# Layer 1's x for three of five groups as wide rows read from DRAM, spreads on TensorE for the other two

## The chip, the cores and the metric

The kernel runs on one core of one Trainium2 chip. The metric is the device time of one execution in microseconds (us). Engines are named as in the profile: PE is TensorE, PEld its weight loads, DVE VectorE, ACT ScalarE, POOL GpSimd, SP SyncE; SPq is the queue of DMAs that SP issues.

## What is computed

A recommendation tower with two layers of feature interaction for a batch of 512, 39 features of 16 numbers each:

```python
e = stack([tbl_f[ids[:, f]] for f in range(39)], axis=1)            # 512 x 39 x 16
z0 = einsum('bid,bjd->bdij', e, e).reshape(B, D, 39 * 39)
cur0 = relu(einsum('bdk,kl->bld', z0, W0))                          # L = 128
next_h, direct0 = split(cur0, 2, axis=1)                            # 64 and 64
z1 = einsum('bid,bjd->bdij', e, next_h).reshape(B, D, 39 * 64)
cur1 = relu(einsum('bdk,kl->bld', z1, W1))
z = sum(concatenate([direct0, cur1], axis=1), axis=-1)              # 512 x 192
h = concatenate([z, dense_ctx], axis=1)
y = relu(relu(h @ W_top1 + b_top1) @ W_top2 + b_top2) @ W_top3
```

The change concerns the products of x with h of layer 1 (`z1`).

## The kernel before

The batch is cut into 16 chunks of 32 rows, so a chunk has N = 32 x 16 = 512 columns. For each chunk POOL issues 11 indirect gathers (L233) into `found`. ACT and DVE split `found` in a high and a low part (`split`, L245 and L328), SP writes both to DRAM (`lay_out`, L193) and reads them back in another layout into `x_parts` (`place`, L205). Three buffers of each (BUFS) let POOL run ahead; gathers of chunk c wait for the split of chunk c-3.

Layer 0 of a chunk: PE adds pairs of features (`add_up`, L408, "sums"), ACT squares them (L252), PE multiplies by the weights (`contract0`, L418), ACT writes the result to `h` (L259, L260).

Layer 1 of a chunk has G = 5 groups, each with QUADS = 4 tiles of 128 rows (two features by 64 rows of h). For group n PE copies the features to all partitions by four matmuls with a 0/1 matrix into the PSUM tensor `spread` (`spread_out`, L429). DVE multiplies it by h into z (`multiply`, L340). For four of five groups ACT rounds z to z_hi (`high_part`, L276) and DVE takes z_lo = z - z_hi (`low_part`, L348); PE multiplies z_hi by two parts of the weights (`contract1_hi`, L440 and L441) and z_lo by one (`contract1_lo`, L448). The fifth group goes in one piece (`contract1_whole`, L456).

There is no scheduler. Each engine runs its own list in the order of the code, and semaphores tie them. In step n PE issues the spread of group n+1, a piece of layer 0 of the next chunk, the low part of group n-1 and the high part of n. DVE does z of n+1, then z_lo of n; in step 0 of a chunk the split of the chunk after next stands between them, in steps 1 and 4 a reduce (L359, L353). SP goes through the chunks: lay_out, place. After the last chunk comes the top network (L500 on). In the code, `multiplied` counts the z that are done, `spread_done` the spreads, `placed` the DMAs of x_parts.

Of the kernel before, what the change touches and what calls it, by code (L numbers as in the profile page):

```python
# [15 lines left out]
P = 128  # L16
B = 512
F = 39
# [24 lines left out]

G = 5
T1 = G * QUADS
SPREAD_FROM = [0, 20, 10, 30]
# [32 lines left out]
def build(nc, ids, base, table, select, w0a, w0b, mix, w1, wt1, bt1, wt2, bt2, wt3, dense, out):  # L79
    with ExitStack() as ctx:  # L80
# [15 lines left out]
        x_rows = nc.dram_tensor("x_rows", (BUFS, 2, F, N), F32, kind="Internal")  # L96
        x_parts = sb("x_parts", [P, BUFS, N], F32R)

        select_sb = sb("select_sb", [P, T0 + G, P], F32R)
# [11 lines left out]
        select_in = staging[:, 0:(T0 + G) * P]  # L111
        w0b_sb = staging[:, (T0 + G) * P:(2 * T0 + G) * P]
# [41 lines left out]
        placed = [sem(f"placed_{b}") for b in range(BUFS)]  # L154
        summed = sem("summed")
# [28 lines left out]
        def _(sp):  # L184
            def lay_out(c):

                b = c % BUFS
                sp.wait_ge(found_lo_done, c + 1)
# [7 lines left out]
            def place(c):  # L196
# [3 lines left out]
                if c >= BUFS:  # L200
                    sp.wait_ge(spread_done, G * (c - BUFS + 1))
                    sp.wait_ge(summed, ND * (c - BUFS + 1))
                for q, f in enumerate(QSTART):
# [3 lines left out]
                                 ).then_inc(placed[b], 16)  # L207

# [8 lines left out]
            for c in range(CHUNKS):  # L217
                lay_out(c)
                place(c)
# [5 lines left out]
        def _(pool):  # L225
            pool.wait_ge(rows_ready, 1)
            for c in range(CHUNKS):
                b = c % BUFS
                if c >= BUFS:

                    pool.wait_ge(found_lo_done, c - BUFS + 1)
                for s in range(SLOTS):
# [89 lines left out]
        def _(dve):  # L322
# [8 lines left out]
            def multiply(n):  # L331
# [3 lines left out]
                dve.wait_ge(spread_done, n + 1)  # L335
# [4 lines left out]
                nc.vector.tensor_tensor(z[:, n % RING], spread[:, :, :],  # L340
# [57 lines left out]
        def _(pe):  # L398
# [23 lines left out]
            def spread_out(n):  # L422

                c, g = n // G, n % G
                if n:
                    pe.wait_ge(multiplied, n)
                for q in range(QUADS):
                    rows = slice(32 * q, 32 * q + 32)
                    last = nc.tensor.matmul(spread[:, q, :], select_sb[rows, T0 + g, :], x_parts[rows, c % BUFS, :],  # L429
# [39 lines left out]
            spread_out(0)  # L469
# [5 lines left out]
            for c in range(CHUNKS):  # L475
                for g in range(G):
                    n = G * c + g
                    if n + 1 < G * CHUNKS:
                        spread_out(n + 1)
# [40 lines left out]
def layout(inputs):  # L520
# [13 lines left out]
    select = np.zeros((P, T0 + G, P), np.float32)  # L534
# [16 lines left out]
    for g in range(G):  # L551
        for q in range(QUADS):
            for a in range(2):
                f = SPREAD_FROM[q] + 2 * g + a
                if f < F:
                    row = 32 * q + 2 * (f - QSTART[q])
                    select[row:row + 2, T0 + g, HALF * a:HALF * a + HALF] = 1.0
                    w1[HALF * a:HALF * a + HALF, QUADS * g + q] = from_w1[f]

    def by_tile(a):  # L560
# [6 lines left out]
        "select": select.reshape(P, (T0 + G) * P),  # L567
# [26 lines left out]
```

## Time and profile before

| | us |
|---|---|
| median of 3 runs (482.2 to 483.02) | 482.69 |
| the profiled execution | 482.86 |
| its span | 480.7 |
| PE busy | 434.3 (90%) |
| DVE busy | 350.1 (73%) |
| POOL busy | 247.9 (52%) |
| ACT busy | 227.4 (47%) |

The busy times are shares of the span of one profiled execution; the 2.2 us between its span and its time lie around the program. Busy times of engines overlap, and an engine's share says nothing of a single stretch: for that there are the windows and timeline views.

### The profile page before, as it was taken

The page shows a single profiled execution, that of the slowest core. Times are in us where ns is not written, and L with a number is a line of the kernel's source. Part 1 is how long each engine was busy: PE and PEld are TensorE (multiplying, and loading weights), DVE is VectorE, ACT ScalarE, POOL GpSimd, SP SyncE. Part 2 cuts the span into 40 slices and gives each one's busy share as a digit, 9 for nine tenths or more (in the row PEclk, how much of TensorE's full clock was granted, in tenths as well). Part 3 has the DMA queues.
Part 4 walks back from the last instruction along what each step waited for, and adds up shares of the span by engine and source line. Part 5 has one row for each costly group of instructions (what it writes and reads, how often), then busy time and mean ns, then how long its engine had stood idle before and what let it go on. Part 6 is the DMA issues. An engine that isn't in the chain of part 4 may idle for free.

```text
span 480.7 us, 4397 instructions
## 1 busy us (share of the span) xinstructions
PE 434.3 (90%) x1618; PEld 244.7 (51%) x1618; DVE 350.1 (73%) x197; ACT 227.4 (47%) x218; POOL 247.9 (52%) x180
## 2 busy tenths in 40 slices
PE   0244699999999999999999999999999999998798
PEld 0211265565656564646555556555565656564453
DVE  0300567988988888888888889797988988887900
ACT  3011633737464645554545546363737464643303
POOL 5877788888888585858585858677000000000000
PEclk9998599999999999999999999999999999998999
DMA  8212010101010100101010101010101010000000
GB/s 295 73 33 39 13 36 4 40 7 40 5 29 17 27 17 16 28 15 26 12 31 5 38 5 40 4 38 6 35 0 37 0 36 1 0 1 1 0 0 2
DMA packets 15563, 12.61 MB, mean 26 GB/s; under 512 B 6352, under 2 KB 12629, under 8 KB 15414
## 3 DMA queue, kind: packets, MB, share of 16 engines
q1 hardware_dynamic: 9204, 9.14, 6.7%
q0 software_dynamic: 5632, 1.35, 3.4%
q10 hardware_dynamic: 706, 1.84, 1.1%
q8 instruction: 13, 0.21, 0.2%
q14 instruction: 8, 0.07, 0.0%
HBM read 9.74 MB, written 2.56 MB: 26 GB/s over the span
## 4 chain that ended last, share of the span: by engine, by line
PE 88%; DMA 4%; DVE 3%; SPq 1%; issue 1%; ACT 1%; ACTq 0%; DVEq 0%
PE acc L418 23%; PE acc L448 12%; PE acc L440 12%; PE acc L441 12%; PE acc L456 11%; PE spread L429 7%; PE sums L408 6%; DMA mix_sb<-in_mix_dram 3%; PE sums L509 1%; DVE z L340 1%; DVE z_lo L348 1%; DMA x_parts<-x_rows 1%; PE spread L502 1%; PE spread L500 1%; SPq L193 1%
## 5 line engine op out<-in xcount | busy, mean ns | idle before, releaser
L233 POOL DMA_INDIRECT found<-in_table_dram,rows_sb x176 | 247.7, 1408 | 86.6 <-issue 51.2
L340 DVE TENSOR_TENSOR z<-spread,h 128x2048 f32<-128x2048 f32 x80 | 183.2, 2290 | 71.3 <-PE spread L429 55.8
L348 DVE TENSOR_TENSOR z_lo<-z,z_hi 128x2048 fp32r<-128x2048 f32 x64 | 146.2, 2284 | 0.0
L276 ACT ACTIVATE z_hi<-z 128x2048 fp32r<-128x2048 f32 x64 | 122.5, 1913 | 41.2 <-DVE z L340 41.2
L418 PE MATMUL acc<-squares,w 128*128 128x512 f32 x224 | 116.6, 638 | 0.0
L440 PE MATMUL acc<-z_hi,w_hi 128*128 128x512 f32 x256 | 103.0, 402 | 2.1 <-ACT z_hi L276 2.1
L441 PE MATMUL acc<-z_hi,w_lo 128*128 128x512 f32 x256 | 101.2, 395 | 0.0
L448 PE MATMUL acc<-z_lo,w_hi 128*128 128x512 f32 x256 | 90.5, 475 | 3.9 <-DVE z_lo L348 3.9
L252 ACT ACTIVATE squares<-sums 128x1024 f32<-128x1024 f32 x64 | 58.7, 917 | 48.6 <-PE sums L408 48.3
L448 PEld LDWEIGHTS acc<-z_lo,w_hi 128*128 128x128 f32 x256 | 47.2, 190 | 36.5 <-issue 22.0
L440 PEld LDWEIGHTS acc<-z_hi,w_hi 128*128 128x128 f32 x256 | 48.6, 190 | 21.9 <-issue 11.2
L418 PEld LDWEIGHTS acc<-squares,w 128*128 128x128 f32 x224 | 39.9, 196 | 37.7 <-issue 37.0
L456 PE MATMUL acc<-z,w_sb 128*128 128x512 f32 x128 | 57.5, 592 | 0.0
L441 PEld LDWEIGHTS acc<-z_hi,w_lo 128*128 128x128 f32 x256 | 48.5, 189 | 11.0 <-issue 0.5
L408 PE MATMUL sums<-x_parts,select_sb 64*128 64x512 f32 (+1 forms) x112 | 33.7, 523 | 18.9 <-DMA x_parts<-x_rows 18.5
L269 ACT ACTIVATE cur<-acc 128x512 f32<-128x512 f32 x16 | 9.6, 598 | 84.1 <-PE acc L456 84.1
L429 PE MATMUL spread<-x_parts,select_sb 32*128 32x512 f32 x320 | 41.4, 505 | 3.8 <-DVE z L340 3.8
L456 PEld LDWEIGHTS acc<-z,w_sb 128*128 128x128 f32 x128 | 24.3, 190 | 24.3 <-issue 23.0
L429 PEld LDWEIGHTS spread<-x_parts,select_sb 32*128 32x128 f32 x320 | 15.6, 185 | 39.8 <-issue 39.4
L259 ACT ACTIVATE h<-acc 64x512 f32<-64x512 f32 x16 | 9.5, 593 | 49.1 <-PE acc L418 49.1
L408 PEld LDWEIGHTS sums<-x_parts,select_sb 64*128 64x128 f32 (+1 forms) x112 | 12.5, 192 | 37.0 <-issue 28.0
L328 DVE TENSOR_TENSOR found_lo<-found,found_hi 117x176 fp32r<-117x176 f32 x16 | 5.5, 341 | 18.8 <-ACT found_hi L245 18.8
(30 smaller groups left out, 93.7 us busy)
## 6 DMA issues: line engine op xcount, KB each, us to landing
x_parts<-x_rows SPq DMA_DIRECT2D x64, 64.0 KB, 2.2
found<-in_table_dram,rows_sb POOLq DMA_INDIRECT x176, 2.4
w_sb<-in_w_dram SPq DMA_DIRECT2D x1, 1280.0 KB, 6.8
x_rows<-found_hi SPq DMA_DIRECT2D x32, 26.8 KB
x_rows<-found_lo SPq DMA_DIRECT2D x32, 26.8 KB
z<-in_select_dram ACTq DMA_DIRECT2D x1, 768.0 KB, 7.6
wt_sb<-in_wt_dram SPq DMA_DIRECT2D x1, 512.0 KB
w<-in_w0a_dram ACTq DMA_DIRECT2D x1, 448.0 KB, 9.7
```

The costliest lines, as they stand in the source:

```text
L233: pool.indirect_dma_start(out=found[:, b, s * D:s * D + D], out_offset=None, in_=table, in_offset=bass.IndirectOffsetOnAxis(ap=rows_sb[:, ...
L252: nc.scalar.activation(squares[:, q % RING0, 0:n, :], sums[:, 0:n, :], ACT.Square).then_inc(squared, 1)
L276: nc.scalar.activation(z_hi[:, n % RING], z[:, n % RING], ACT.Copy).then_inc(hi_done, 1)
L340: nc.vector.tensor_tensor(z[:, n % RING], spread[:, :, :], h[:, c % 2, :].unsqueeze(1).to_broadcast([P, QUADS, N]), ALU.mult).then_inc(mul ...
L348: nc.vector.tensor_tensor(z_lo[:, n % RING], z[:, n % RING], z_hi[:, n % RING], ALU.subtract).then_inc(lo_done, 1)
L408: last = nc.tensor.matmul(sums[:, a, :], select_sb[rows, t, :], x_parts[rows, c % BUFS, :], start=True, stop=True)
L418: last = nc.tensor.matmul(acc0[:, :], w0[:, t, :], squares[:, q % RING0, a, :], start=(t == 0), stop=(t == T0 - 1))
L429: last = nc.tensor.matmul(spread[:, q, :], select_sb[rows, T0 + g, :], x_parts[rows, c % BUFS, :], start=True, stop=True)
L440: nc.tensor.matmul(acc1[:, :], w1_hi[:, t, :], z_hi[:, r, a, :], start=(t == 0), stop=False)
L441: last = nc.tensor.matmul(acc1[:, :], w1_lo[:, t, :], z_hi[:, r, a, :], start=False, stop=False)
L448: last = nc.tensor.matmul(acc1[:, :], w1_hi[:, QUADS * g + a, :], z_lo[:, r, a, :], start=False, stop=False)
L456: last = nc.tensor.matmul(acc1[:, :], w1_sb[:, VT + a, :], z[:, r, a, :], start=False, stop=(a == QUADS - 1))
```

## The change

`found` itself, neither high nor low part, is now also written to DRAM (`x_rows[b, 2]`), in three more DMAs of `lay_out`. For groups 0, 2 and 4 of a chunk (WIDE) SP reads four features at a time from there as one row of 2048 numbers, with a stride of zero for 64 partitions, into one half of `x_wide`; two such DMAs of 512 KB make a group's x (`widen`). x_wide has one buffer for each of the three groups, so `widen` for chunk c+1 waits until that group's z of chunk c is done. DVE's `multiply` takes `x_wide` in place of `spread` for these groups. Groups 1 and 3 (SPREAD) still go through PE, now two steps ahead. Features are dealt to groups anew, and the matrices of `layout` follow. The gathers wait for the new write of `found` as well.

```diff
--- before.py
+++ after.py
@@ -41,9 +41,13 @@
 ND = len(DUOS)
 
 
+
 G = 5
 T1 = G * QUADS
-SPREAD_FROM = [0, 20, 10, 30]
+SPREAD = [1, 3]
+WIDE = [0, 2, 4]
+SPREAD_FROM = [0, 24, 12, 36]
+WIDE_FROM = [[4, 8], [16, 20], [28, 32]]
 
 VT = (G - 1) * QUADS
 VG = G - 1
@@ -93,10 +97,11 @@
         found = sb("found", [GP, BUFS, GW])
         found_hi = sb("found_hi", [GP, BUFS, GW], F32R)
         found_lo = sb("found_lo", [GP, BUFS, GW], F32R)
-        x_rows = nc.dram_tensor("x_rows", (BUFS, 2, F, N), F32, kind="Internal")
+        x_rows = nc.dram_tensor("x_rows", (BUFS, 3, F, N), F32, kind="Internal")
+        x_wide = sb("x_wide", [P, len(WIDE), QUADS * N])
         x_parts = sb("x_parts", [P, BUFS, N], F32R)
 
-        select_sb = sb("select_sb", [P, T0 + G, P], F32R)
+        select_sb = sb("select_sb", [P, T0 + len(SPREAD), P], F32R)
         w0 = sb("w0", [P, T0, P])
         mix_sb = sb("mix_sb", [P, T0, F])
         w1_sb = sb("w1_sb", [P, T1, P])
...
@@ -185,6 +192,13 @@
             def lay_out(c):
 
                 b = c % BUFS
+                if c >= BUFS:
+                    for i in range(len(WIDE)):
+                        sp.wait_ge(wide_in[i], 32 * (c - BUFS + 1))
+                sp.wait_ge(gathered[b], 16 * SLOTS * uses(c))
+                for s, w in enumerate(SET_COLS):
+                    sp.dma_start(x_rows[b, 2, :, GW * s:GW * s + w],
+                                 found[F * s:F * s + F, b, 0:w]).then_inc(full_out[b], 16)
                 sp.wait_ge(found_lo_done, c + 1)
                 if c >= BUFS:
                     sp.wait_ge(placed[b], 16 * QUADS * uses(c - BUFS))
@@ -198,13 +212,25 @@
                 b = c % BUFS
                 sp.wait_ge(rows_out[b], 16 * 6 * uses(c))
                 if c >= BUFS:
-                    sp.wait_ge(spread_done, G * (c - BUFS + 1))
+                    sp.wait_ge(spread_done, len(SPREAD) * (c - BUFS + 1))
                     sp.wait_ge(summed, ND * (c - BUFS + 1))
                 for q, f in enumerate(QSTART):
                     start = x_rows[b, 0, f, 0:1]
                     sp.dma_start(x_parts[32 * q:32 * q + 32, b, :].bitcast(F32),
                                  bass.AP(start.tensor, start.offset, [[N, QF], [F * N, 2], [1, N]])
                                  ).then_inc(placed[b], 16)
+
+            def widen(c, i):
+
+                b = c % BUFS
+                if i == 0:
+                    sp.wait_ge(full_out[b], 16 * SETS * uses(c))
+                if c:
+                    sp.wait_ge(multiplied, G * (c - 1) + WIDE[i] + 1)
+                for a, f in enumerate(WIDE_FROM[i]):
+                    sp.dma_start(x_wide[HALF * a:HALF * a + HALF, i, :],
+                                 x_rows[b, 2, f:f + QUADS, :].rearrange("f n -> (f n)").unsqueeze(0)
+                                 .to_broadcast([HALF, QUADS * N])).then_inc(wide_in[i], 16)
 
             sp.dma_start(ids_sb[:, :], ids).then_inc(ids_in, 16)
             sp.dma_start(w1_sb[:, :, :], w1).then_inc(w1_in, 16)
@@ -214,9 +240,20 @@
                              (wt2_sb[:, :, :], wt2), (wt3_sb[:, :], wt3), (bt1_sb[:, :], bt1),
                              (bt2_sb[:, :], bt2), (feat_b[HALF:, :], dense)):
                 sp.dma_start(dst, src).then_inc(mlp_in, 16)
-            for c in range(CHUNKS):
-                lay_out(c)
-                place(c)
+            lay_out(0)
+            place(0)
+            for i in range(len(WIDE)):
+                widen(0, i)
+            lay_out(1)
+            place(1)
+            for c in range(CHUNKS - 1):
+                widen(c + 1, 0)
+                if c + 2 < CHUNKS:
+                    lay_out(c + 2)
+                widen(c + 1, 1)
+                if c + 2 < CHUNKS:
+                    place(c + 2)
+                widen(c + 1, 2)
             sp.wait_ge(y_ready, 1)
             sp.dma_start(out, y_sb[:, :]).then_inc(out_done, 16)
             sp.wait_ge(out_done, 16)
@@ -229,6 +266,7 @@
                 if c >= BUFS:
 
                     pool.wait_ge(found_lo_done, c - BUFS + 1)
+                    pool.wait_ge(full_out[b], 16 * SETS * uses(c - BUFS))
                 for s in range(SLOTS):
                     pool.indirect_dma_start(
                         out=found[:, b, s * D:s * D + D], out_offset=None, in_=table,
@@ -229,6 +266,7 @@
                 if c >= BUFS:
 
                     pool.wait_ge(found_lo_done, c - BUFS + 1)
+                    pool.wait_ge(full_out[b], 16 * SETS * uses(c - BUFS))
                 for s in range(SLOTS):
                     pool.indirect_dma_start(
                         out=found[:, b, s * D:s * D + D], out_offset=None, in_=table,
@@ -332,12 +370,17 @@
                 c, g = n // G, n % G
                 if g == 0:
                     dve.wait_ge(h_ready, 2 * (c + 1))
-                dve.wait_ge(spread_done, n + 1)
+                if g in SPREAD:
+                    dve.wait_ge(spread_done, len(SPREAD) * c + SPREAD.index(g) + 1)
+                    x = spread[:, :, :]
+                else:
+                    dve.wait_ge(wide_in[WIDE.index(g)], 32 * (c + 1))
+                    x = x_wide[:, WIDE.index(g), :].rearrange("p (t n) -> p t n", n=N)
                 if n >= RING and is_v(n - RING):
                     dve.wait_ge(lo_done, v_count(n - RING))
                 elif n >= RING:
                     dve.wait_ge(contracted1, n - RING + 1)
-                nc.vector.tensor_tensor(z[:, n % RING], spread[:, :, :],
+                nc.vector.tensor_tensor(z[:, n % RING], x,
                                         h[:, c % 2, :].unsqueeze(1).to_broadcast([P, QUADS, N]),
                                         ALU.mult).then_inc(multiplied, 1)
 
@@ -421,12 +464,12 @@
 
             def spread_out(n):
 
-                c, g = n // G, n % G
-                if n:
-                    pe.wait_ge(multiplied, n)
+                c, i = n // G, SPREAD.index(n % G)
+                if c or i:
+                    pe.wait_ge(multiplied, G * c + SPREAD[i - 1] + 1 if i else G * (c - 1) + SPREAD[-1] + 1)
                 for q in range(QUADS):
                     rows = slice(32 * q, 32 * q + 32)
-                    last = nc.tensor.matmul(spread[:, q, :], select_sb[rows, T0 + g, :], x_parts[rows, c % BUFS, :],
+                    last = nc.tensor.matmul(spread[:, q, :], select_sb[rows, T0 + i, :], x_parts[rows, c % BUFS, :],
                                             start=True, stop=True)
                 last.then_inc(spread_done, 1)
 
@@ -466,7 +509,7 @@
             pe.wait_ge(select_ready, 1)
             add_up(0)
             pe.wait_ge(w0_ready, 3)
-            spread_out(0)
+            spread_out(SPREAD[0])
             for d in range(ND):
                 add_up(d + 1)
                 contract0(d)
...
@@ -475,8 +518,8 @@
             for c in range(CHUNKS):
                 for g in range(G):
                     n = G * c + g
-                    if n + 1 < G * CHUNKS:
-                        spread_out(n + 1)
+                    if (n + 2) % G in SPREAD and SPREAD[0] < n + 2 < G * CHUNKS:
+                        spread_out(n + 2)
                     if c + 1 < CHUNKS and g < ND:
                         if ND * (c + 1) + g + 1 < ND * CHUNKS:
                             add_up(ND * (c + 1) + g + 1)
...
@@ -548,14 +591,18 @@ def layout
-    for g in range(G):
+    for i, g in enumerate(SPREAD):
...
+    for i, g in enumerate(WIDE):
+        for a in range(2):
+            f = WIDE_FROM[i][a]
+            w1[HALF * a:HALF * a + HALF, QUADS * g:QUADS * g + QUADS] = from_w1[f:f + QUADS].transpose(1, 0, 2)
```

How the lists of the engines stand before and after. First PE in a step without a spread now (step 2 of a chunk): the last weight product of one group up to the low part of the next. Before:

```order
L441 MATMUL acc<-z_hi,w_lo 128x512
L429 MATMUL spread<-x_parts,select_sb 128x512 [waits multiplied]
L429 MATMUL spread<-x_parts,select_sb 128x512 x3
L408 MATMUL sums<-x_parts,select_sb 128x512 [waits squared]
L418 MATMUL acc<-squares,w 128x512 [waits squared]
L418 MATMUL acc<-squares,w 128x512
L448 MATMUL acc<-z_lo,w_hi 128x512 [waits lo_done]
L448 MATMUL acc<-z_lo,w_hi 128x512 x3
```

And in the changed kernel:

```order
L484 MATMUL acc<-z_hi,w_lo 128x512
L451 MATMUL sums<-x_parts,select_sb 128x512 [waits squared]
L461 MATMUL acc<-squares,w 128x512 [waits squared]
L461 MATMUL acc<-squares,w 128x512
L491 MATMUL acc<-z_lo,w_hi 128x512 [waits lo_done]
L491 MATMUL acc<-z_lo,w_hi 128x512 x3
```

The four spread matmuls between L441 (now L484) and the sums are gone; nothing took their place.

Then DVE for one chunk, from the split (L328, now L366) to the z of the next chunk's second group. Before:

```order
L328 TENSOR_TENSOR found_lo<-found,found_hi 117x176 [waits rows_out_1,found_hi_done]
L348 TENSOR_TENSOR z_lo<-z,z_hi 128x2048 [waits contracted1,hi_done]
L340 TENSOR_TENSOR z<-spread,h 128x2048 [waits contracted1,spread_done]
L348 TENSOR_TENSOR z_lo<-z,z_hi 128x2048 [waits contracted1,hi_done]
L359 TENSOR_REDUCE feat_a<-cur 128x32 [waits evicted1]
L340 TENSOR_TENSOR z<-spread,h 128x2048 [waits lo_done,spread_done]
L348 TENSOR_TENSOR z_lo<-z,z_hi 128x2048 [waits hi_done]
L340 TENSOR_TENSOR z<-spread,h 128x2048 [waits lo_done,spread_done]
L348 TENSOR_TENSOR z_lo<-z,z_hi 128x2048 [waits contracted1,hi_done]
L340 TENSOR_TENSOR z<-spread,h 128x2048 [waits lo_done,spread_done,h_ready]
L353 TENSOR_REDUCE feat_b<-direct 64x32 [waits evicted0]
L340 TENSOR_TENSOR z<-spread,h 128x2048 [waits lo_done,spread_done]
```

And in the changed kernel (L383 is z, L391 z_lo):

```order
L366 TENSOR_TENSOR found_lo<-found,found_hi 117x176 [waits rows_out_1,found_hi_done]
L391 TENSOR_TENSOR z_lo<-z,z_hi 128x2048 [waits contracted1,hi_done]
L383 TENSOR_TENSOR z<-x_wide,h 128x2048 [waits contracted1,wide_in_1]
L391 TENSOR_TENSOR z_lo<-z,z_hi 128x2048 [waits contracted1,hi_done]
L402 TENSOR_REDUCE feat_a<-cur 128x32 [waits evicted1]
L383 TENSOR_TENSOR z<-spread,h 128x2048 [waits lo_done,spread_done]
L391 TENSOR_TENSOR z_lo<-z,z_hi 128x2048 [waits hi_done]
L383 TENSOR_TENSOR z<-x_wide,h 128x2048 [waits lo_done,wide_in_2]
L391 TENSOR_TENSOR z_lo<-z,z_hi 128x2048 [waits contracted1,hi_done]
L383 TENSOR_TENSOR z<-x_wide,h 128x2048 [waits lo_done,wide_in_0,h_ready]
L396 TENSOR_REDUCE feat_b<-direct 64x32 [waits evicted0]
L383 TENSOR_TENSOR z<-spread,h 128x2048 [waits lo_done,spread_done]
```

The order is the same. Three of five z now read `x_wide` and wait for its DMAs (wide_in), so that z_lo, z, z_lo with all inputs in SBUF follow on one another twice in a chunk, before the first reduce and before the next z of group 0.

Last, SP's queue. Before, for one chunk:

```order
L193 DMA x_rows<-found_hi 39x176 [waits placed_1,found_lo_done]
L193 DMA x_rows<-found_hi 39x176
L193 DMA x_rows<-found_hi 39x160
L193 DMA x_rows<-found_lo 39x176 x2
L193 DMA x_rows<-found_lo 39x160
L205 DMA x_parts<-x_rows 32x1x512 [waits summed,spread_done,rows_out_1]
L205 DMA x_parts<-x_rows 32x1x512 x3
```

And in the changed kernel, the middle of a chunk, from the writes of high and low parts:

```order
L207 DMA x_rows<-found_hi 39x176 [waits placed_1,found_lo_done]
L207 DMA x_rows<-found_hi 39x176
L207 DMA x_rows<-found_hi 39x160
L207 DMA x_rows<-found_lo 39x176 x2
L207 DMA x_rows<-found_lo 39x160
L231 DMA x_wide<-x_rows 64x2048 [waits multiplied]
L231 DMA x_wide<-x_rows 64x2048
L219 DMA x_parts<-x_rows 32x1x512 [waits summed,spread_done,rows_out_1]
L219 DMA x_parts<-x_rows 32x1x512 x3
L231 DMA x_wide<-x_rows 64x2048 [waits multiplied]
L231 DMA x_wide<-x_rows 64x2048
L231 DMA x_wide<-x_rows 64x2048 [waits multiplied,full_out_1]
```

The reads of x_parts (L205, now L219) now stand behind a pair of wide reads that waits for a z of the running chunk.

## Rows read from the trace of the kernel before

**Rows 1.** The page: busy time, share of the span and instructions of each engine.

```profile
PE 434.3 (90%) x1618; PEld 244.7 (51%) x1618; DVE 350.1 (73%) x197; ACT 227.4 (47%) x218; POOL 247.9 (52%) x180
```

**Rows 2.** The page: the chain that ended last, by engine and by line.

```profile
PE 88%; DMA 4%; DVE 3%; SPq 1%; issue 1%; ACT 1%; ACTq 0%; DVEq 0%
PE acc L418 23%; PE acc L448 12%; PE acc L440 12%; PE acc L441 12%; PE acc L456 11%; PE spread L429 7%; PE sums L408 6%; DMA mix_sb<-in_mix_dram 3%; PE sums L509 1%; DVE z L340 1%; DVE z_lo L348 1%; DMA x_parts<-x_rows 1%; PE spread L502 1%; PE spread L500 1%; SPq L193 1%
```

**Rows 3.** Windows view, one chunk: busy time by engine, PEclk, DMA share, GB/s.

```profile
200.12:225.36 25.24, 25.24 (x99) 14.41 (x98) 21.61 (x12) 13.63 (x13) 17.61 (x12) 1.00 0.11 20
```

**Rows 4.** The gathers' line, whole span, then up to 57.8: duration min/median/max, starts.

```profile
L233 POOL DMA_INDIRECT found<-in_table_dram,rows_sb x176: 992/996/2978, 3.8 to 333.8; - x176
...
DMA to landing us min/median/max: 2.2/2.4/6.8
...
L233 POOL DMA_INDIRECT found<-in_table_dram,rows_sb x40: 992/996/2521, 3.8 to 56.8; - x40
```

**Rows 5.** Timeline, PE, chunk in the middle: start, duration, engine, line, what.

```profile
200.12 0.51 PE L429 MATMUL spread<-x_parts,select_sb 32*128 32x512 f32 x4
...
200.56 0.50 PE L408 MATMUL sums<-x_parts,select_sb 64*128 64x512 f32 x2
```

**Rows 6.** Timeline: SP and PE at the start; DVE, PE in the last chunk.

```profile
25.67 2.52 SPq L205 DMA_DIRECT2D x_parts<-x_rows  x4
...
41.02 1.14 SPq L193 DMA_DIRECT2D x_rows<-found_hi  x3
...
55.32 0.80 PE L429 MATMUL spread<-x_parts,select_sb 32*128 32x512 f32 x4 [3.77 <-DVE z L340]
...
432.24 2.28 DVE L340 TENSOR_TENSOR z<-spread,h 128x2048 f32<-128x2048 f32 x1
...
437.49 2.29 DVE L340 TENSOR_TENSOR z<-spread,h 128x2048 f32<-128x2048 f32 x1 [2.39 <-PE spread L429]
...
458.01 1.45 PE L456 MATMUL acc<-z,w_sb 128*128 128x512 f32 x3
```

**Rows 7.** Timeline, DVE: a z_lo and the z behind it.

```profile
212.84 2.29 DVE L348 TENSOR_TENSOR z_lo<-z,z_hi 128x2048 fp32r<-128x2048 f32 x1
...
215.04 2.29 DVE L340 TENSOR_TENSOR z<-spread,h 128x2048 f32<-128x2048 f32 x1
```

**Rows 8.** Groups by line and shape, DVE: count, busy us, mean ns, idle before.

```profile
L340 DVE TENSOR_TENSOR z<-spread,h 128x2048 f32<-128x2048 f32 x80 | 183.2, 2290 | 71.3 <-PE spread L429 55.8 <-ACT h L260 11.9 <-issue 3.7
L348 DVE TENSOR_TENSOR z_lo<-z,z_hi 128x2048 fp32r<-128x2048 f32 x64 | 146.2, 2284 | 0.0
...
L353 DVE TENSOR_REDUCE feat_b<-direct 64x32 f32<-64x512 f32 x16 | 10.7, 668 | 0.0
```

**Rows 9.** Windows view at the start, then the page's DMA issues (us to landing).

```profile
5.00:9.00 4.00, 0.00 (x0) 0.00 (x0) 0.00 (x0) 0.00 (x0) 2.98 (x3) 1.00 0.99 400
...
x_parts<-x_rows SPq DMA_DIRECT2D x64, 64.0 KB, 2.2
...
w_sb<-in_w_dram SPq DMA_DIRECT2D x1, 1280.0 KB, 6.8
```

**Rows 10.** Timeline, POOL and DVE: gathers beside z_lo.

```profile
86.63 1.00 POOL L233 DMA_INDIRECT found<-in_table_dram,rows_sb  x1 [0.30 <-issue]
86.64 2.31 DVE L348 TENSOR_TENSOR z_lo<-z,z_hi 128x2048 fp32r<-128x2048 f32 x1
...
91.08 2.28 DVE L348 TENSOR_TENSOR z_lo<-z,z_hi 128x2048 fp32r<-128x2048 f32 x1
...
91.42 2.80 POOL L233 DMA_INDIRECT found<-in_table_dram,rows_sb  x1 [0.30 <-issue]
```

**Rows 11.** Timeline, DVE and POOL at the start: two operations back to back.

```profile
19.33 2.27 DVE L374 TENSOR_TENSOR w_lo<-w_sb,w_hi 128x2048 fp32r<-128x2048 f32 x1
...
20.20 2.52 POOL L233 DMA_INDIRECT found<-in_table_dram,rows_sb  x1 [0.30 <-issue]
21.52 0.32 DVE L328 TENSOR_TENSOR found_lo<-found,found_hi 117x176 fp32r<-117x176 f32 x1
```

More of the change, by code:

```diff
@@ L110, in build @@
         staging = z[:, :, :, :].rearrange("p r a n -> p (r a n)")
-        select_in = staging[:, 0:(T0 + G) * P]
-        w0b_sb = staging[:, (T0 + G) * P:(2 * T0 + G) * P]
+        select_in = staging[:, 0:(T0 + len(SPREAD)) * P]
+        w0b_sb = staging[:, (T0 + len(SPREAD)) * P:(2 * T0 + len(SPREAD)) * P]
         h = sb("h", [P, 2, N])
@@ L154, in build @@
         placed = [sem(f"placed_{b}") for b in range(BUFS)]
+        full_out = [sem(f"full_out_{b}") for b in range(BUFS)]
+        wide_in = [sem(f"wide_in_{i}") for i in range(len(WIDE))]
         summed = sem("summed")
@@ L533, in layout @@
     w0a, w0b = np.zeros((2, T0 * P, P), np.float32)
-    select = np.zeros((P, T0 + G, P), np.float32)
+    select = np.zeros((P, T0 + len(SPREAD), P), np.float32)
     mix = np.zeros((T0 * P, F), np.float32)
@@ L550, in layout @@
     from_w1 = np.asarray(inputs["L0_rec_W1"]).reshape(F, HALF, P)
-    for g in range(G):
+    for i, g in enumerate(SPREAD):
         for q in range(QUADS):
             for a in range(2):
-                f = SPREAD_FROM[q] + 2 * g + a
+                f = SPREAD_FROM[q] + 2 * i + a
                 if f < F:
                     row = 32 * q + 2 * (f - QSTART[q])
-                    select[row:row + 2, T0 + g, HALF * a:HALF * a + HALF] = 1.0
+                    select[row:row + 2, T0 + i, HALF * a:HALF * a + HALF] = 1.0
                     w1[HALF * a:HALF * a + HALF, QUADS * g + q] = from_w1[f]
+    for i, g in enumerate(WIDE):
+        for a in range(2):
+            f = WIDE_FROM[i][a]
+            w1[HALF * a:HALF * a + HALF, QUADS * g:QUADS * g + QUADS] = from_w1[f:f + QUADS].transpose(1, 0, 2)
     def by_tile(a):
@@ L566, in layout @@
         "table": np.concatenate(tables),
-        "select": select.reshape(P, (T0 + G) * P),
+        "select": select.reshape(P, (T0 + len(SPREAD)) * P),
         "w0a": by_tile(w0a),
```

## Prediction

> **What bounds the kernel now.** I read the page's shares first: PE is busy 434.3 us of 480.7, DVE 350.1, POOL 247.9 [rows 1]. The chain of work that ended last is 88% PE, and 7% of the span in it are the spreads of L429 [rows 2]. Then one chunk in the middle: from one spread at 200.12 to the same spread a chunk later the windows view gives 25.24 us, with PE busy for all of them, DVE for 21.61, and the clock at its upper level throughout [rows 3]. So each PE instruction taken out of this stretch shortens the period, as long as DVE (21.61) and what feeds DVE do not become the longer chain. The feeder that matters is POOL: 11 gathers per chunk, 176 in all, the last at 333.8 [rows 4]. They are ahead of need here, so their slowness costs nothing today.
>
> **What is removed.** Three of five spreads in each chunk. In the timeline a spread starts at 200.12 and the sums behind it at 200.56 [rows 5]; its slot is 0.44 us, and without it the sums stand where it stood. Three slots are 1.32 us, so a chunk bound by PE takes 25.24 − 1.32 = 23.92 us. The PE order excerpt shows such a slot gone and nothing put in its place.
>
> **The last chunk.** It has no layer 0 of a next chunk beside it. Its first z starts at 432.24, but the second one only at 437.49, after 2.39 us of waiting for a spread, and the matmuls on its last z (L456) start at 458.01 [rows 6]. After the change that spread is issued two steps ahead, so DVE runs through: five z and four z_lo at 2.20 from start to start (212.84 to 215.04 in [rows 7]), 19.8, and two reduces of 0.67 [rows 8]. That ends at 432.24 + 21.1 = 453.4; with the four z_lo matmuls (an estimate, 0.95) L456 starts at 454.3 instead of 458.01. I take 3.5 us.
>
> **The start.** h of chunk 0 waits for x_parts of chunk 1, and in front of these the SP queue now has six wide DMAs, 3.15 MB (each 64 x 2048 x 4 bytes). At 193 GB/s (w_sb, 1.31 MB landed in 6.8 us) they take 16 us, at 400 GB/s (window 5 to 9) 8 us [rows 9]. They can issue from 28.2 on (x_parts of chunk 0: 25.67 and 2.52), and x_rows of chunk 1 issue at 41.02 [rows 6], so the delay is 0 to 3 us. Against it, PE no longer waits 3.77 us for the first z to issue the second spread at 55.32, for 0.80 at the slow clock [rows 6]; I put some 1.5 us on that. I take nothing, and 2 us either way for the range.
>
> **Costs that lie beside other work.** The wide DMAs move 3.15 MB per chunk: 7.9 us at the one rate, 16.3 at the other, both below 23.92. The next x for a group is asked for when its z is done and is needed nearly a chunk later. x_parts of chunk c+2 now stand on SP's queue behind the wait for the third z. That z ends at 217.33 (215.04 + 2.29) [rows 7], the sums that need them start a period after 200.56, at 225.80. In between: six issues of some 0.6 (2.52 for four, [rows 6]), and 2.2 to land [rows 9], or 5.4 us for 1.05 MB at the slow rate and 2.2; 7.6 of 8.5. Hidden, but with less than a microsecond of room at the slow rate, which DVE's greater lead widens. The extra copy (three writes of x_rows) issues while the split runs. z from SBUF should take the same time: z from PSUM and z_lo, both of whose inputs are in SBUF, take 2290 and 2284 ns [rows 8].
>
> **What is added and does cost: three more DVE operations with both inputs in SBUF.** Look at gathers beside DVE. Beside z (an input in PSUM), a reduce, or nothing, a gather takes 1.00. One that starts during z_lo does not finish: z_lo 91.08 to 93.36, gather 91.42 to 94.22, which is 0.86 after z_lo's end [rows 10]. Every long gather in the trace (up to 2978 ns [rows 4]) ends 0.86 to 0.88 behind such an operation. The same rows give a gather when free a start every 1.30 (1.00 and 0.30 between). Today four operations per chunk do this; then seven, since x_wide and h are both in SBUF. And they stand back to back (DVE excerpt): z_lo, z, z_lo without a gap, twice in a chunk.
>
> Whether a waiting gather slips in at the seam of two such operations is not shown in steady state. The nearest row is at the start: L374 ends at 21.60, the short L328 runs on to 21.84, and the gather that began at 20.20 ends at 22.72 [rows 11]. That is 0.88 behind the second, 1.12 behind the first: it did not get in. Against it stands a gather at 86.63 that was not held though z_lo began at 86.64 [rows 10]; it came fresh at a seam, and did not wait through one. The Trainium skill (SBUF — State Buffer, section "Who interferes with whom") says that a DVE instruction with two SBUF inputs contends with a GpSimd instruction that reads SBUF, and that whoever issues first has the shared ports for the whole instruction. The first part agrees with every held gather here. By the second I would expect the gather to take its turn at the seam, which is rival B; the gather at 20.20 speaks against it.
>
> **The sum if gathers are held through seams.** Count from the split found_lo (0.26 start to start), then DVE's order at 2.20 each: z_lo, z, z_lo end at 6.96; reduce and the spread-fed z are free until 9.7; z_lo, z, z_lo end at 16.4; a gap of about 0.26 (the z with three waits); wide z to 18.95; then reduce and z from spread to 21.75, and from there DVE waits for the next split. Gathers get in at 6.96, 8.13, 9.43; at 16.4; at 18.95, 20.12, and then each 1.30. Without a stall that is 3 + 1 + 4 = 8 in 23.92, where 11 are needed. To have 11, seven must come after 18.95: 18.95 + 1.17 + 5 x 1.30 = 26.6 at least, 27.9 when the eighth would fit; the middle is 27.3. Such a chunk is 27.3 − 25.24 = 2.06 longer than now (bounds 1.4 and 2.7).
>
> How many chunks: at 57.8, near the split that needs gather 33, gather 40 was issued [rows 4], a lead of seven. A chunk at 23.92 uses up three: two more periods run at 23.9 and 24.7, then eleven at 27.3, until the last gathers; two more at 23.92. Sum: 11 x 2.06 = 22.7, less 0.5, less 3 x 1.32 = 4.0, less 3.5 for the last chunk: +14.7. The profiled execution took 482.86 us, 0.17 over the median of the three, so 497.6; I say **498**. With periods of 26.6 to 27.9 it is 490 to 504, and with the start 488 to 506; a PE that waits long enough in one piece to lose its clock could add some microseconds (at the lower level the four spread matmuls of 55.32 took 0.80, those of 200.12 0.51 [rows 5, 6]), so 488 to 510 for this case. PE's waits should come in pieces of 1 to 2 us, so I expect little of it.
>
> **Rivals.**
> - **B, gathers get in at seams.** Then each of the seven operations lets one through: ends at 2.54, 4.75, 6.96, free 8.13 and 9.43, ends at 12.0, 14.2, 16.4, 18.95, free 20.12, 21.42, 22.72: 12 in 23.92, enough for 11. PE stays the bound: 15 periods x 1.32 = 19.8, and 3.5: 482.9 − 23.3 = 459.6, say **460**, 456 to 464 with the start. It decides at one gather each 23.92/11 = 2.17 us. For it: the fresh gather at 86.63 and the lock's wording. Against: the one at 20.20.
> - **C, the wide DMAs are slow**, since 64 readers fetch the same 8 KB. The turning point is 3.15 MB and some 0.3 of others in 25.24 us, 137 GB/s. At a quarter of the 400 GB/s a chunk takes 34.5 us, 9.3 x 16 = 149 us more. The trace has no read with zero stride; rows of 10 KB went at 193 and more. By the Trainium skill (the same page, section "Door 1: The DMA port swizzle") 64 partitions reach 8 of 16 ports, half of some 436 GB/s: 14.5 us a chunk, hidden.
> - **D, the gain is given back halfway**: single seams let gathers through, or x_parts land late behind the wide ones and stall PE a microsecond per chunk. Anything between: 470 to 495, middle near 482.
>
> **Chances.** Held through seams 0.52; B 0.28; C 0.07; D 0.13, of which 0.04 faster, 0.03 the same, 0.06 slower. A measurement here tells apart about 0.2%, 1 us. Faster 0.32, same 0.03, slower 0.65. The range has to reach both main cases: 456 to 510.
>
> **What the profile after would show.** Right: gathers of 4 to 7 us that end 0.87 behind the second or third operation of a block; L366 or the ACT split waiting for found; POOL busy for nearly all the span and gathering until beyond 400; a period near 27.3 until then and 23.9 after; z from x_wide at 2.29. B: no gather over some 3 us, ends behind the first operation, period 23.9. C: waits of z for x_wide, DMA share near 1. Wrong in the size: if the second gather after a release takes longer than 1.30, or wide DMAs delay the gathers' landing (they took up to 6.8 us under load at the start [rows 4]).

## The result and the profile after

The changed kernel takes 486.82 us (median of 7 runs, 484.06 to 488.32) against 482.69 (7 runs, 482.2 to 483.28). The ratio is 1.0073 with an interval of 1.0042 to 1.0104: slower by 0.7%, on the side that was forecast, but by 4 us and not by 15. That lies in the whole range (456 to 510), but outside 488 to 510, which belonged to the main case. Its times scatter more widely than those of the kernel before.

The page of the kernel after, its line of busy times and the chain that ended last, by engine and by line:

```profile
PE 414.9 (86%) x1426; PEld 238.0 (49%) x1426; DVE 346.5 (71%) x197; ACT 226.8 (47%) x218; POOL 257.7 (53%) x180
...
PE 37%; DMA 20%; DVE 15%; SPq 10%; ACT 7%; issue 6%; POOL 5%; ACTq 0%; DVEq 0%; POOLq 0%
DMA x_parts<-x_rows 16%; PE acc L499 11%; DVE z L383 7%; PE acc L491 7%; DVE z_lo L391 7%; ACT z_hi L314 6%; SPq L219 5%; POOL found L271 5%; PE acc L461 4%; PE acc L483 4%; PE acc L484 4%; SPq L231 3%; DMA found<-in_table_dram,rows_sb 2%; PE sums L451 2%; DMA x_rows<-found_lo 2%
```

PE is busy 19 us less than in [rows 1], and yet the execution is longer. The chain has gone from 88% PE [rows 2] to 37%: it now passes through DMA, DVE, SP's queue and ACT, and its largest item is the DMA of x_parts, 16%. POOL stands at 5%. One chunk in the middle, in the windows view (engines in the order PE, PEld, DVE, ACT, POOL; then PEclk, DMA share, GB/s):

```profile
189.20:214.90 25.70, 23.95 (x87) 13.92 (x85) 21.42 (x12) 13.59 (x14) 17.42 (x12) 1.00 0.71 148
```

It answers to [rows 3]: 25.70 instead of 25.24, and no engine is busy throughout. PE idles for 1.75 us of it, DVE for 4.3. The timeline of the same chunk, rows of ACT, DVE, SP's queue and PE (start, duration, engine, line; in brackets the idle time ahead and what ended it):

```profile
189.01 0.60 ACT L307 ACTIVATE cur<-acc 128x512 f32<-128x512 f32 x1 [4.88 <-PE acc L499]
...
189.51 1.90 ACT L314 ACTIVATE z_hi<-z 128x2048 fp32r<-128x2048 f32 x1
...
191.31 0.34 ACT L283 ACTIVATE found_hi<-found 117x176 fp32r<-117x176 f32 x1
...
191.68 0.34 DVE L366 TENSOR_TENSOR found_lo<-found,found_hi 117x176 fp32r<-117x176 f32 x1 [4.11 <-ACT found_hi L283]
...
191.94 2.29 DVE L391 TENSOR_TENSOR z_lo<-z,z_hi 128x2048 fp32r<-128x2048 f32 x1
...
194.14 2.28 DVE L383 TENSOR_TENSOR z<-x_wide,h 128x2048 f32<-128x2048 f32 x1
...
196.45 1.09 SPq L231 DMA_DIRECT2D x_wide<-x_rows  x2
...
197.65 2.48 SPq L219 DMA_DIRECT2D x_parts<-x_rows  x4
...
205.41 0.51 PE L451 MATMUL sums<-x_parts,select_sb 64*128 64x512 f32 x2 [1.53 <-DMA x_parts<-x_rows]
```

Read it as a chain. PE ends the last product of the chunk before, ACT evicts it (189.01), then rounds z (189.51) and splits found (191.31); DVE, idle for 4.11 us by then, does its split, a z_lo and the third z, which ends at 196.42. Only then may SP issue the second pair of wide reads, and behind these x_parts (197.65 to 200.13). They land at about 205.4, and PE has waited 1.53 us for them. From there it takes PE 9.2 us to the end of its last product, and the loop closes: 16.5 + 9.2 = 25.7, the period. PE has this wait in 13 chunks, 0.8 to 1.9 us each. Who waited, and how long DMAs took from issue to landing (waits view, then the page's DMA issues):

```profile
DVE found_lo L366 <- ACT found_hi L283: 74.0, 14, 21.2
...
PE sums L451 <- DMA x_parts<-x_rows: 40.0, 15, 12.1
```

```profile
x_wide<-x_rows SPq DMA_DIRECT2D x96, 512.0 KB, 6.6
x_parts<-x_rows SPq DMA_DIRECT2D x64, 64.0 KB, 5.8
```

x_parts took 2.2 us in [rows 9] and take 5.8 now, with a megabyte of wide rows ahead of them in the same queue; the first two experiments test that this is the reason. The wide pair that is issued from 196.45 lands after (view of the tile x_wide from 196.4 to 197.2):

```profile
DMA to landing us min/median/max: 5.0/6.0/7.0
```

So the first of the pair lands at 201.45, the second, issued at 196.95, at 203.97, and the last of x_parts 1.4 us behind it.

**POOL was not the brake.** Its gathers beside DVE's operations, in the timeline of the same chunk:

```profile
194.80 2.50 POOL L271 DMA_INDIRECT found<-in_table_dram,rows_sb  x1 [5.24 <-DMA x_rows<-found]
...
203.54 2.29 DVE L383 TENSOR_TENSOR z<-x_wide,h 128x2048 f32<-128x2048 f32 x1
...
204.79 1.90 POOL L271 DMA_INDIRECT found<-in_table_dram,rows_sb  x1 [0.30 <-issue]
...
205.74 2.29 DVE L391 TENSOR_TENSOR z_lo<-z,z_hi 128x2048 fp32r<-128x2048 f32 x1
```

z from x_wide runs from 203.54 to 205.83 and z_lo follows without a gap at 205.74. The gather that began at 204.79 ends at 206.69, which is 0.86 behind the *first* of them. It got in at the seam. From the first z on, 47 gathers were waiting when one operation with two SBUF inputs followed another (44 times without a gap, 3 times with 0.2 us); all 47 ended 0.86 to 0.87 us behind the first. The line of the gathers:

```profile
L271 POOL DMA_INDIRECT found<-in_table_dram,rows_sb x176: 992/998/3109, 3.8 to 343.9; - x176
```

Against [rows 4] the last one starts 10 us later, the longest takes 3109 ns. POOL has time left: 17.42 busy of the 25.70 above. Where it idles in this chunk, before 194.80, it waits for the new write of `found`, which stands behind wide reads on SP's queue. From the third split on ACT never waits for a gather, so this costs nothing.

**Where the 4.3 us of span are.** The first z begins 4.8 us later than before, at 57.67 instead of 52.88. But the first chunk is then 4.4 us shorter (21.98 against 26.34), since its z hardly wait for spreads; the second chunk's first z is only 0.4 late. Of the two kernels, before and after, DVE:

```profile
52.88 2.29 DVE L340 TENSOR_TENSOR z<-spread,h 128x2048 f32<-128x2048 f32 x1 [11.89 <-ACT h L260]
...
79.22 2.29 DVE L340 TENSOR_TENSOR z<-spread,h 128x2048 f32<-128x2048 f32 x1 [0.26 <-issue]
```

```profile
79.66 2.29 DVE L383 TENSOR_TENSOR z<-x_wide,h 128x2048 f32<-128x2048 f32 x1 [1.12 <-ACT h L298]
...
462.31 3.59 PE L499 MATMUL acc<-z,w_sb 128*128 128x512 f32 x8
```

The loss is in the 14 chunks from there to the last one's first z: 357.9 us, 25.57 a chunk, where it had been 353.0 (to 432.24 in [rows 6]), 25.22 a chunk; that is 4.9. The last chunk takes 1.1 less (its first z starts at 437.59 and L499 at 462.31; in [rows 6] 432.24 and 458.01). Rows of the changed kernel's start, of SP, ACT, PE and DVE:

```profile
28.27 3.79 SPq L231 DMA_DIRECT2D x_wide<-x_rows  x6
...
42.64 0.35 ACT L283 ACTIVATE found_hi<-found 117x176 fp32r<-117x176 f32 x1 [2.25 <-DMA found<-in_table_dram,rows_sb]
...
45.06 1.20 SPq L207 DMA_DIRECT2D x_rows<-found_lo  x3
...
49.34 2.49 SPq L219 DMA_DIRECT2D x_parts<-x_rows  x4
...
53.54 0.79 PE L451 MATMUL sums<-x_parts,select_sb 64*128 64x512 f32 x2 [12.06 <-DMA x_parts<-x_rows]
...
57.67 2.29 DVE L383 TENSOR_TENSOR z<-x_wide,h 128x2048 f32<-128x2048 f32 x1 [14.31 <-ACT h L298]
```

Two steps are slower than before. The gathers of chunk 1 land later: ACT splits at 42.64, and SP writes the high part from 43.82 instead of 41.02. And x_parts are issued only at 49.34, 3.1 us behind the last write of x_rows (46.26), where it had been 1.1. The third step, from there to PE's sums at 53.54, takes 4.2 us in both kernels.

### The profile page after: what moved, and what is told of

It reads as the page before. It is cut to its first block, busy times and chain, and to the rows that moved or that the text cites. A ratio compares the mean times of both kernels' runs of the same rounds, so it can differ in the third digit from the quotient of the medians.

```text
span 485.0 us, 4211 instructions
## 1 busy us (share of the span) xinstructions
PE 414.9 (86%) x1426; PEld 238.0 (49%) x1426; DVE 346.5 (71%) x197; ACT 226.8 (47%) x218; POOL 257.7 (53%) x180
## 4 chain that ended last, share of the span: by engine, by line
PE 37%; DMA 20%; DVE 15%; SPq 10%; ACT 7%; issue 6%; POOL 5%; ACTq 0%; DVEq 0%; POOLq 0%
DMA x_parts<-x_rows 16%; PE acc L499 11%; DVE z L383 7%; PE acc L491 7%; DVE z_lo L391 7%; ACT z_hi L314 6%; SPq L219 5%; POOL found L271 5%; PE acc L461 4%; PE acc L483 4%; PE acc L484 4%; SPq L231 3%; DMA found<-in_table_dram,rows_sb 2%; PE sums L451 2%; DMA x_rows<-found_lo 2%
## 5 line engine op out<-in xcount | busy, mean ns | idle before, releaser
L271 POOL DMA_INDIRECT found<-in_table_dram,rows_sb x176 | 257.5, 1463 | 86.9 <-issue 51.2
L391 DVE TENSOR_TENSOR z_lo<-z,z_hi 128x2048 fp32r<-128x2048 f32 x64 | 146.2, 2284 | 5.8 <-ACT z_hi L314 5.8
L383 DVE TENSOR_TENSOR z<-x_wide,h 128x2048 f32<-128x2048 f32 x48 | 109.7, 2286 | 17.6 <-ACT h L298 17.6
L484 PE MATMUL acc<-z_hi,w_lo 128*128 128x512 f32 x256 | 101.9, 398 | 0.0
L383 DVE TENSOR_TENSOR z<-spread,h 128x2048 f32<-128x2048 f32 x32 | 72.9, 2278 | 0.5 <-PE spread L472 0.5
L451 PE MATMUL sums<-x_parts,select_sb 64*128 64x512 f32 (+1 forms) x112 | 32.2, 512 | 43.5 <-DMA x_parts<-x_rows 40.0
L366 DVE TENSOR_TENSOR found_lo<-found,found_hi 117x176 fp32r<-117x176 f32 x16 | 5.4, 340 | 74.0 <-ACT found_hi L283 74.0
L499 PE MATMUL acc<-z,w_sb 128*128 128x512 f32 x128 | 57.5, 592 | 0.0
L484 PEld LDWEIGHTS acc<-z_hi,w_lo 128*128 128x128 f32 x256 | 49.1, 192 | 11.1 <-issue 0.5
L499 PEld LDWEIGHTS acc<-z,w_sb 128*128 128x128 f32 x128 | 24.3, 190 | 24.4 <-issue 23.0
L506 PE MATMUL acc<-w,mix_sb 128*39 128x128 f32 x14 | 3.2, 420 | 15.6 <-DMA mix_sb<-in_mix_dram 15.6
```

The source lines that it names most:

```text
L271: pool.indirect_dma_start(out=found[:, b, s * D:s * D + D], out_offset=None, in_=table, in_offset=bass.IndirectOffsetOnAxis(ap=rows_sb[:, ...
L383: nc.vector.tensor_tensor(z[:, n % RING], x, h[:, c % 2, :].unsqueeze(1).to_broadcast([P, QUADS, N]), ALU.mult).then_inc(multiplied, 1)
L391: nc.vector.tensor_tensor(z_lo[:, n % RING], z[:, n % RING], z_hi[:, n % RING], ALU.subtract).then_inc(lo_done, 1)
L451: last = nc.tensor.matmul(sums[:, a, :], select_sb[rows, t, :], x_parts[rows, c % BUFS, :], start=True, stop=True)
L484: last = nc.tensor.matmul(acc1[:, :], w1_lo[:, t, :], z_hi[:, r, a, :], start=False, stop=False)
L499: last = nc.tensor.matmul(acc1[:, :], w1_sb[:, VT + a, :], z[:, r, a, :], start=False, stop=(a == QUADS - 1))
```

## The experiments

The theory after this: **a loop** through SP's queue, and x_parts that land behind a megabyte, set the period of 25.7. The rivals: **gathers** (the prediction's), and **bandwidth** (the wide reads as such are too slow).

**x_parts first.** The order of SP's queue, nothing else:

```diff
                 if c + 2 < CHUNKS:
                     lay_out(c + 2)
+                    place(c + 2)
                 widen(c + 1, 1)
-                if c + 2 < CHUNKS:
-                    place(c + 2)
                 widen(c + 1, 2)
```

> SP issues x_parts of chunk c+2 ahead of the second pair of wide reads, nothing else changed. Loop theory (PE's sums wait for x_parts, which wait on SP's queue for the third z and land behind 1 MB of wide data, 5.8 us instead of 2.2): x_parts then land before 203.8 in the chunk of 189 to 215, the stall of 1.5 us goes, and a period falls from 25.7 to about 24, bound by PE again: 460 to 466 us. Gather theory (the prediction's: POOL held off by DVE sets the period): no change, 484 to 488. Bandwidth theory (the wide reads as such are too slow): no change either, or x_wide now late by as much.

Measured: 466.18 us, ratio to the kernel before 0.9671 (0.9646 to 0.9696), at the upper edge of what was expected. A chunk takes 24.1 us, between equal matmuls of two chunks in PE's timeline:

```profile
191.53 0.39 PE L450 MATMUL sums<-x_parts,select_sb 128*128 128x512 f32 x1
...
215.61 0.39 PE L450 MATMUL sums<-x_parts,select_sb 128*128 128x512 f32 x1
```

and x_parts land in 2.3 us (median; the line under its tile):

```profile
DMA to landing us min/median/max: 2.2/2.3/3.5
```

All wide reads are still there, so bandwidth was not it, and all seven DVE operations are, so gathers were not. The position in the queue is worth 20 us, and PE no longer waits for x_parts in steady state.

**Small wide reads.** The queue of the changed kernel, but after chunk 0 each wide read moves 64 bytes per partition:

```diff
-                    sp.dma_start(x_wide[HALF * a:HALF * a + HALF, i, :],
+                    w = QUADS * N if c == 0 else 16
+                    sp.dma_start(x_wide[HALF * a:HALF * a + HALF, i, 0:w],
...
-                                 .to_broadcast([HALF, QUADS * N])).then_inc(wide_in[i], 16)
+                                 .to_broadcast([HALF, w])).then_inc(wide_in[i], 16)
```

> Every wide read after chunk 0's moves 64 bytes instead of 8 KB per partition, with the same issues, order and waits (x of groups 0, 2 and 4 stays mostly that of chunk 0). Loop theory: the place on the queue alone is not enough, since x_parts issued at 200.1 land at 202.3 without traffic and the sums ask for them at 203.8: the stall goes, 460 to 466 us. If the wait on the queue alone did it: 484 and more. Gather theory: no change.

Measured: 466.23 us (one run), x_parts again land in 2.2, and the chunks take 24.1. So the wait on the queue alone did not cost it either; the two together did. Without the megabyte ahead of them x_parts may be issued late; issued ahead of the megabyte, as in the run before, they do not have to wait for it.

**Wide reads for chunk 0 only**, with x_parts straight behind lay_out:

```diff
-                widen(c + 1, 0)
                 if c + 2 < CHUNKS:
                     lay_out(c + 2)
-                widen(c + 1, 1)
-                if c + 2 < CHUNKS:
                     place(c + 2)
-                widen(c + 1, 2)
...
-                    dve.wait_ge(wide_in[WIDE.index(g)], 32 * (c + 1))
+                    dve.wait_ge(wide_in[WIDE.index(g)], 32)
```

> The wide reads are done for chunk 0 only, x_parts follow lay_out as in the kernel before (x of groups 0, 2 and 4 stays that of chunk 0). DVE still does seven operations per chunk with both inputs in SBUF. Gather theory of the prediction: 495 or more, since nothing else stands in the way of it. Loop theory: gathers get in at the seams of DVE's operations, PE bounds: 456 to 464, and the first z starts at 57.7 still.

Measured: 466.65 us (one run). The gather theory needed 495. The loop theory had 464 at most, a small miss: the chunks took 24.1 here too, not 23.9. The first z starts at 57.08, with the six wide reads of the start still there. The gathers' line shows that POOL kept up:

```profile
L269 POOL DMA_INDIRECT found<-in_table_dram,rows_sb x176: 995/1000/3450, 3.8 to 326.2; - x176
```

Three kernels at 24.1 with quite different DMAs point to a second, shorter loop, one without SP. PE's timeline in the run with x_parts first shows its only wait in a chunk:

```profile
205.95 1.98 PE L460 MATMUL acc<-squares,w 128*128 128x512 f32 x4
...
208.16 0.47 PE L482 MATMUL acc<-z_hi,w_hi 128*128 128x512 f32 x1 [0.23 <-ACT z_hi L313]
...
208.47 0.40 PE L483 MATMUL acc<-z_hi,w_lo 128*128 128x512 f32 x1
```

PE ends its last product, ACT evicts it and only then rounds z, and PE waits for z_hi. DVE idles 2.8 us a chunk here too (it waits for the split, which ACT does after z_hi), but PE does not wait for that.

**ACT's order.**

```diff
-                    if g == 0 and c:
-                        evict1(c - 1)
                     if is_v(n):
                         high_part(n)
                     if g == 0 and c + 2 < CHUNKS:
                         split(c + 2)
+                    if g == 0 and c:
+                        evict1(c - 1)
```

> ACT rounds the first z of a chunk and splits found before it evicts the previous chunk's sum, nothing else changed. Loop theory: the loop runs PE's last product, eviction, z_hi, split, DVE's split, z_lo, z, SP, x_parts, PE's sums; with the eviction off it DVE's 4.1 us of waiting for found_hi falls to about none, x_parts come some 3 us sooner and the stall goes: 460 to 468 us. Theories without this loop: no change, 484 to 488.

Measured: 456.81 us (one run), a larger gain than was expected (460 at best). A chunk in the windows view:

```profile
188.44:212.09 23.65, 23.65 (x86) 14.00 (x85) 21.42 (x13) 13.50 (x14) 20.30 (x12) 1.00 0.72 155
```

23.65 us, and PE busy for all of it: both loops are gone and PE bounds again, though SP's queue is still in the changed kernel's order. DVE no longer waits for found_hi, and x_parts are in time. The rows that answer to those of the run with x_parts first:

```profile
204.72 1.98 PE L461 MATMUL acc<-squares,w 128*128 128x512 f32 x4
...
206.77 0.39 PE L484 MATMUL acc<-z_hi,w_lo 128*128 128x512 f32 x1
```

From the squares' products to the first product with w_lo it takes 2.05 us here and 2.52 there. That is all of the difference between 24.11 and 23.65. The next run gives what the time is to be compared with.

**Control: the kernel before with ACT's new order** (the same edit in that kernel).

> The kernel before, with ACT's new order alone. If PE bounds it, the periods stay 25.24 and only the last chunk gains: 480 to 482.5 us. If the new ACT order were the whole gain of the run with it, this would come to 460.

Measured: 479.89 us, ratio 0.9942 (0.9921 to 0.9964), a hair under the 480 expected. Its chunks take 25.16 instead of 25.24, and the last one 1 us less. Against 25.16 the 23.65 of the run before are 1.51 us less for three spreads, 0.50 each. ACT's order alone gives 2.5 us (482.41 in this comparison). The change itself, with ACT's new order on both sides, gives 23 us: 479.89 to 456.81. In the changed kernel the loops had held that gain back.

**The DMAs of the change without its gain.** The kernel before, all five spreads on PE, with the third plane of x_rows, the wide reads, SP's queue and its waits as in the change; DVE goes on reading `spread`, and SP itself waits for a buffer's last wide read before it issues the next, since DVE does not:

```diff
-            for c in range(CHUNKS):
-                lay_out(c)
-                place(c)
+            lay_out(0)
+            place(0)
+            for i in range(len(WIDE)):
+                widen(0, i)
+            lay_out(1)
+            place(1)
+            for c in range(CHUNKS - 1):
+                widen(c + 1, 0)
+                if c + 2 < CHUNKS:
+                    lay_out(c + 2)
+                widen(c + 1, 1)
...
```

> The kernel before, all five spreads on PE, with the DMAs of the change added in its queue order and its waits; what they bring is not used. Loop theory: the start loses 4.8, the loop of 25.7 to 26 takes the place of 25.24: 492 to 498 us. If the wide reads are hidden as I predicted: 482 to 487 (the start alone).

Measured: 489.8 us, one run, 2 us below the range of the loop theory and 3 above that of hidden reads. The first z starts at 57.81, 4.9 later than before; the chunks take 25.24 where x_parts are in time and up to 26.65 where not, 25.50 on average against 25.29, so 3.2 us in all; the last chunk takes 0.8 less. So the wide reads make x_parts late even where no spread has gone (PE waits for them in six chunks, 0.3 to 1.4 us), but PE's own 25.24 hides most of it, and DVE never waits for ACT's split here. In one chunk:

```profile
189.00:214.70 25.70, 25.37 (x98) 14.41 (x97) 21.60 (x12) 13.61 (x13) 15.50 (x11) 1.00 0.71 146
```

**The start's order.** The changed kernel, with four of the six first wide reads behind x_parts of chunk 1:

```diff
             lay_out(0)
             place(0)
-            for i in range(len(WIDE)):
-                widen(0, i)
+            widen(0, 0)
             lay_out(1)
             place(1)
+            widen(0, 1)
+            widen(0, 2)
```

> The changed kernel, with only the start's queue order new: x_parts of chunk 1 ahead of the last four wide reads. The first z starts at 53 to 54 instead of 57.7, the rest as before: 481 to 485 us. If the gathers or the traffic of two wide reads are what delays the start: above 56, and 485 to 488.

Measured: 483.69 us (one run; the runs of the changed kernel reach from 484.06 to 488.32, so the timeline says more here than the time). DVE's timeline:

```profile
52.04 2.29 DVE L384 TENSOR_TENSOR z<-x_wide,h 128x2048 f32<-128x2048 f32 x1 [11.75 <-ACT h L299]
```

The first z starts 5.6 us sooner than in the changed kernel, and even sooner than in the kernel before (52.88). Here x_parts of chunk 1 are issued 1.1 us behind the last write, as in the kernel before. Of the 5.6 us the span keeps 3.1: the first chunk takes 23.52 instead of 21.98, and the 14 behind it 1.0 more in all.

**All three.** x_parts first, ACT's order, the start's order.

> Parts first on SP's queue, ACT's eviction behind z_hi and split, and at the start x_parts of chunk 1 ahead of four of the six wide reads. If the start lost 4.8 us (first z at 57.7 instead of 52.9) to the queue, it gets 3 to 4 of them back on top of 456.8: 452 to 455 us. If the start was lost to something else (gathers that land later): 456 to 457. The period stays 23.65, bound by PE, since x_parts were no longer late with the new ACT order alone.

Measured: 451.7 us (median of 6 runs, 450.76 to 456.38), ratio 0.9383 (0.9351 to 0.9415), just under the range expected, and so 31 us below the kernel before and 35 below the changed one. It does all the work of the changed kernel, in another order. PE's chunk, in the windows view:

```profile
189.00:212.65 23.65, 23.65 (x86) 14.01 (x85) 21.42 (x13) 13.50 (x13) 20.30 (x12) 1.00 0.77 164
```

## Why the prediction was right or wrong

The forecast was 498 us, 15 more than before; the kernel took 4 more. That it came out slower, as forecast, was luck: the term of 22.7 us that made it slower in the sum was nothing, and what did make it slower stood in the sum at nothing.

- **What bounds it, and the gain per spread**: right that PE bounds and that each slot out of it shortens a chunk. The slot was read as 0.44 us from start to start (0.44 x 3 = 1.32). The slot is 0.50: where PE bounds again, a chunk takes 23.65 us, 1.51 less than the same order of ACT gives the kernel before.
- **"it did not get in"**: this step failed, and with it the main case, gathers held through seams and chunks of 27.3 us (11 x 2.06 = 22.7 us). One gather at the start, held past the short L328, was carried over to seams in steady state. In the changed kernel 47 of 47 gathers got in at them, and the longest took 3.1 us. Rival B had this right.
- **"Hidden, but with less than a microsecond of room at the slow rate, which DVE's greater lead widens"**: the second step that failed, and the one that decided. I gave x_parts 7.6 us of 8.5. Both figures were off. The 7.6 was the time of the wide pair alone, and for that it was right (196.45 to 203.97, 7.5); x_parts' own rows come behind it and take 1.4 more, so it is 9.0 from 196.42 to 205.41, which would not have fitted into 8.5 either (PE waits for x_parts in six chunks even with all five spreads and the change's DMAs). And the sums were due sooner: two of the three slots taken out lie between that z and the sums, so 8.47 became 7.5 (203.88, which is 205.41 less the 1.53 of waiting). The change itself took away a microsecond of the room that its own DMAs needed. DVE's lead did not grow, since ACT does not split before it has evicted, and that waits for PE: DVE idles 4.1 us in each chunk (there is no such wait of L328 in the chunk of [rows 3], where DVE ran 21.61 of 25.24 and waited for spreads). So a hidden path taken at nothing cost more than the whole gain: 25.7 us a chunk, where 23.92 was forecast without gathers in the way and 23.65 came out once the loops were gone.
- **Rival D** named it: x_parts late behind the wide reads, a microsecond of PE per chunk, 470 to 495. It had a chance of 0.13, far too little for a path with 0.9 us of room by my own sum.
- **The start**: a delay of 0 to 3 us and a gain of 1.5 against it were taken, so nothing. Both were too small: the first z is 4.8 late, and the first chunk is then 4.4 shorter. They nearly cancel, and by the second chunk's first z the kernel is 0.4 us behind the one before (1.8 behind the forecast, which had 1.32 of gain in that chunk), within the 2 us allowed. The delay is in two steps in a row, the gathers and the writes of x_rows; I had counted the queue's traffic once.
- **The last chunk**: 3.5 taken, 1.1 measured. DVE waits 2.42 us there for z_hi, since ACT evicts first and waits for PE; this was not in the chain that I wrote down. With ACT's order new, L499 begins 22.2 us behind the last chunk's first z, which is the 22.1 that I had added up; it is 24.7 in the changed kernel and 25.8 in the kernel before.
- **z from SBUF at the time of z from PSUM**: right, 2286 and 2278 ns. **Rival C**: wrong, the reads with zero stride ran well enough.

## What to carry to other kernels

When work is taken off the engine that bounds, redo the sum of every hidden path with the time that is left: here the change took 1.0 of 8.5 us, on a path thought to have 0.9 to spare. Add up such a path to the last byte that is waited for, not to that of the large DMA ahead of it. DMAs that are needed soon go ahead of large ones that are needed late in the same queue, and an in-order engine should not wait for the bound engine ahead of work that others wait for. Before a change is dropped as useless, look at who waits now: here 35 us lay behind three changes of order.

## What was not expected of the hardware

- A gather that waits for a DVE operation with two SBUF inputs got in at the seam to the next one 47 times of 47 in the changed kernel, but not always elsewhere. In the run with ACT's new order it was held through one seam in 12 chunks, always at the first z_lo behind the split, and so in 12 chunks of the run with all three; in the control four were held at the seam from found_lo to z_lo. The timeline of the run with ACT's new order, DVE and POOL:

```profile
203.15 2.28 DVE L391 TENSOR_TENSOR z_lo<-z,z_hi 128x2048 fp32r<-128x2048 f32 x1
...
203.97 4.54 POOL L271 DMA_INDIRECT found<-in_table_dram,rows_sb  x1 [0.30 <-issue]
...
205.35 2.27 DVE L383 TENSOR_TENSOR z<-x_wide,h 128x2048 f32<-128x2048 f32 x1
```

  It ends at 208.51, 0.89 behind the second operation. By the Trainium skill (SBUF — State Buffer, section "Who interferes with whom") a DVE instruction with two SBUF inputs contends with a GpSimd instruction that reads SBUF, and issue order decides who blocks. The first agrees with every gather held here; the second agrees with the 47 and not with the 12. What tells the seams apart stays open. It costs nothing here, since PE is busy throughout.
- Wide reads into 64 partitions move about half of the 400 GB/s at 0.99 of the loads to 128 partitions [rows 9]. Windows view of the changed kernel's start, with the six wide reads on the queue:

```profile
32.00:36.00 4.00, 4.00 (x6) 1.32 (x6) 0.00 (x0) 1.02 (x1) 2.99 (x3) 1.00 1.00 208
```

  That is 208 GB/s with the DMA engines busy throughout; the 148 at a share of 0.71 in a chunk come to the same. The Trainium skill (SBUF — State Buffer, section "Door 1: The DMA port swizzle") says that 64 partitions reach half of the 16 ports, some 218 of 436 GB/s; this agrees. So the stride of zero cost little or nothing on top.
